# Attention in a fused transformer block: P·V in two halves around the score pairs, and a fourth of the maximum search handed to ScalarE and a scan

## Chip, cores and metric

The kernel runs on one core of a Trainium2 chip, as one program. The metric is the device time of one execution in microseconds (us); lower is better. What is compared is the median of several executions.

## What is computed

The reference is a "macaron" block on x of shape (8, 2048, 256): half a routed feed-forward step, attention, half a routed feed-forward step. The change touches the attention alone, which in the reference is

```python
q = _lowrank(xh, Uq, Vq, bq)
k = _lowrank(xh, Uk, Vk, bk)
v = _lowrank(xh, Uv, Vv, bv)
scores = jnp.einsum('bqhd,bkhd->bhqk', q, k) / DH ** 0.5
attn = jax.nn.softmax(scores, axis=-1)
out = jnp.einsum('bhqk,bkhd->bqhd', attn, v)
```

with 8 batches, 8 heads of 32, and 2048 queries and keys.

## The kernel before

`macaron_block` runs eight stages one after the other. The attention stage `attend` is by far the longest and lies between about 880 and 4370 us of the trace.

**Tiling.** A unit is 512 queries of one group of four heads in one batch. There are 64 units. Within a unit the scores are computed with keys on the partitions and queries along the free dimension, as 16 chunks of 128 keys by four heads: 64 score tiles of 128x512. TensorE writes them into two PSUM banks in turn (`ps_s`), ScalarE takes the exponential of each into `probs` in SBUF, and TensorE multiplies each chunk of four tiles by V into one accumulating bank (`ps_acc`). This last product is called P.V; its four heads are four matmuls that run side by side in four column groups of the array. For chunks 13 and 15 (`RAW_CHUNKS`) TensorE also sums the probabilities into `ps_misc` by a matmul with ones; for the others GpSimd adds them up (`pool_sum`), partly with the help of accumulating DMAs, and one more matmul (`close_z`) adds that sum.

**The maximum.** Softmax subtracts the row maximum before the exponential. It enters the score matmul as an extra row of q, so it must be known a unit ahead. For this the unit's scores are computed once more with queries on the partitions: `max_four` does it for 128 queries, 512 keys and four heads at a time, in four PSUM banks (`ps_max`, one per head), and VectorE reduces the four banks to their maxima (`part_max`). There are 16 such steps per unit, numbered n, run four ahead (`MAX_LEAD`); n modulo 4 is the quarter of the keys, called c in that code. `ps_max` is single, so step n waits until VectorE has finished step n-1 (`part_max_done`), in line 1581.

**The order on TensorE** is written out by hand in `batch`. A unit has 16 cycles, i = 0 to 15, of four score tiles each. This text calls the first two tiles of a cycle A1 and A2, the next two B1 and B2, the maximum step M, and P.V of the previous chunk PV. A cycle is A1, A2, PV, B1, B2, M. Each score tile waits until the exponential of the tile two before it is done, since there are two banks. Some cycles hold more: cycle 3 `close_z`, cycle 4 `turn_z`, cycle 6 `turn_o` (four transposes each), cycle 13 `turn_max`, which takes the place of A2 for a moment. Cycle 0 works off chunk 15 of the unit before.

**ScalarE** takes exponentials in the order of the tiles, and copies `ps_acc` after tile 1 and `ps_misc` after tile 15. **VectorE** does one reduction per cycle (line 1457), a reciprocal in cycle 4 and a normalisation in cycle 6. **GpSimd** adds chunks (line 1437) and starts DMAs that add one chunk to another (line 1414); such a start waits for `pv_done` of the pair's second chunk.

Of the kernel before, what the change touches and what calls it, by code (L numbers as in the profile page):

```python
# [15 lines left out]
P = 128  # L16
# [1196 lines left out]
def attend(nc, tag, qk, v_dram, out):  # L1213
# [6 lines left out]
    FOURS = TILES // HG  # L1220
    BU = NG * NU
# [21 lines left out]
    with ExitStack() as ctx:  # L1243
# [19 lines left out]
        neg_max = sb("neg_max", [P, HG * QT])  # L1263
        max_row = sb("max_row", [HG * QT, P], F32R)
# [19 lines left out]
        part_max_done = sem("part_max_done")  # L1284
        neg_max_done = sem("neg_max_done")
# [159 lines left out]
        def _(dve):  # L1445
# [3 lines left out]

            def part_max_of(unit, n, first_unit=False):  # L1450

                if n == 0 and not first_unit:

                    dve.wait_ge(neg_max_done, unit)
                t, c = divmod(n, QT)
                dve.wait_ge(max_scores, unit * FOURS + n + 1)
                nc.vector.reduce_max(part_max[:, :, t, c], ps_max[:], AX.X).then_inc(part_max_done, 1)  # L1457
                if n == FOURS - 1:
                    dve.wait_ge(part_max_done, unit * FOURS + FOURS)
                    if not first_unit:  # L1460

                        dve.wait_ge(max_turned, unit)
                    nc.vector.tensor_reduce(neg_max[:], part_max[:].rearrange("p h t c -> p (h t) c"), AX.X, ALU.max,
                                            negate=True).then_inc(neg_max_done, 1)
# [47 lines left out]
        def _(act):  # L1512
# [6 lines left out]

            row_of_max(0, 1, first_unit=True)  # L1520

            def batch(b, first_batch=False, last=False):
                for un in range(BU):
# [27 lines left out]
                    for j in range(TILES):  # L1551
                        c, h = divmod(j, HG)
                        if h == 0 and (carry or c >= RING):
                            free(c)
                        act.wait_ge(scores, unit * TILES + j + 1)
                        nc.scalar.activation(probs[:, c % RING, h], ps_s[:, j % 2], ACT.Exp, scale=SCALE  # L1556
                                             ).then_inc(exp_done, 1)
                        if carry and j == 1:
                            copy_acc(unit)
                        if carry and j == CLOSE_Z_IN * PER_CYC + 3:  # L1560
                            copy_z(unit)
                        if j == TURN_MAX_IN * PER_CYC and (un + 1 < BU or not last):
                            row_of_max(unit + 1, 1)
# [11 lines left out]
        def _(pe):  # L1575
            def scores_for_max(unit, un, n, first_unit=False):

                t, c = divmod(n, QT)
                if n >= 1 or not first_unit:

                    pe.wait_ge(part_max_done, unit * FOURS + n)
                for h in range(HG):
# [22 lines left out]
            def batch(b, first_batch=False, last=False):  # L1605
                for un in range(BU):
# [4 lines left out]
                    def pv(n, k, c):  # L1611

                        if c == 0 and carry:

                            pe.wait_ge(oT_done, n)
                        for h in range(HG):
                            last = nc.tensor.matmul(ps_acc[h * DH:(h + 1) * DH, :],  # L1617
                                                    v[:, k // NU, c, h * DH:(h + 1) * DH], probs[:, c % RING, h],
                                                    start=(c == 0), stop=(c == NC - 1))
                        if c in RAW_CHUNKS:  # L1620
                            if c == RAW_CHUNKS[0] and carry:

                                pe.wait_ge(o_done, n)
                            for h in range(HG):
                                last = nc.tensor.matmul(ps_misc[h * DH:(h + 1) * DH, :], ones[:, 0:DH],  # L1625
                                                        probs[:, c % RING, h], start=(c == RAW_CHUNKS[0]), stop=False)
                        last.then_inc(pv_done, 1)

                    def close_z(n, k):

                        pe.wait_ge(pool_added, n * ADDS + ADDS)
                        for h in range(HG):
                            last = nc.tensor.matmul(ps_misc[h * DH:(h + 1) * DH, :], ones[:, 0:DH],
                                                    pool_sum[:, k % 2, h], start=False, stop=True)
                        last.then_inc(z_done, 1)
# [35 lines left out]
                    for i in range(NCYC):  # L1671
# [15 lines left out]
                        if i > 0:  # L1687
                            pv(unit, un, i - 1)
                        elif carry:
                            pv(unit - 1, (un - 1) % BU, NC - 1)  # L1690
                        if carry and i == CLOSE_Z_IN:
                            close_z(unit - 1, un - 1)
                        if turning:
                            pe.wait_ge(max_row_done, unit + 2)
                            score(j + 1)
                        for n in range(2, PER_CYC):

                            pe.wait_ge(exp_done, unit * TILES + j + n - 1)
                            score(j + n)
                        if carry and i == TURN_Z_IN:  # L1700
                            turn_z(unit)
                        if carry and i == TURN_O_IN:
                            turn_o(unit)
                        max_four(i)
                if last:
                    pe.wait_ge(exp_done, (b * BU + BU) * TILES)
                    pv(b * BU + BU - 1, BU - 1, NC - 1)
                    close_z(b * BU + BU - 1, BU - 1)
# [60 lines left out]
```

## Time and profile before

| | us |
|---|---|
| median of 3 executions | 4966.07 (4965.32 to 4968.26) |
| the profiled execution | 4967.85 |
| its span, first to last instruction | 4965.8 |
| TensorE busy in the span | 3964.8 (80%) |
| VectorE busy | 3282.3 (66%) |
| ScalarE busy | 2837.2 (57%) |
| GpSimd busy | 2799.9 (56%) |

The span is divided among stages with different limits. The shares of the whole tell little of the attention stage, in which all the rows below were taken. Matmuls overlap, so what a matmul costs is read from the distance between the starts of neighbours and not from its own duration.

### The profile page before, as it was taken

The numbers are of one execution on the slowest core, as the hardware profiler recorded it, in microseconds if no ns is written. First come the engines' busy times: TensorE is split into PE (matmuls) and PEld (weight loads), VectorE is DVE, ScalarE is ACT, GpSimd is POOL, SyncE is SP. The second block draws the span as 40 slices with busy tenths as digits, with TensorE's granted clock in tenths as the row PEclk, the third lists the DMA queues.
The fourth block names the chain that finished last, engine by engine and source line by source line (L and its number), as shares of the span: only waits on it lengthen the run. The fifth ranks groups of instructions, "written<-read, shape, count | busy, mean of one in ns | idle before, by whom it ended". The sixth has DMA issues, their size and how long they took to land. (4 is left out here: it accounts for less than half of the span.)

```text
span 4965.8 us, 69030 instructions
## 1 busy us (share of the span) xinstructions
PE 3964.8 (80%) x21362; PEld 1556.9 (31%) x21362; DVE 3282.3 (66%) x3736; ACT 2837.2 (57%) x5622; POOL 2799.9 (56%) x966
## 2 busy tenths in 40 slices
PE   0156476599999999999999999999999999910266
PEld 0134354133333333333333333333333333300144
DVE  8744365677767767767776776777677777469644
ACT  4143355266666666666666666666666666623043
POOL 0011000377777877777787777778777777743111
PEclk9999788699999999999999999999999999955598
DMA  6200499557667665756756676675756764566200
GB/s 221 78 26 5 157 352 326 117 110 154 129 143 152 131 143 115 162 125 136 161 121 141 128 158 132 135 157 107 158 125 142 158 128 101 116 197 213 76 5 5
DMA packets 316558, 676.10 MB, mean 136 GB/s; under 512 B 24780, under 2 KB 208608, under 8 KB 268832
## 3 DMA queue, kind: packets, MB, share of 16 engines
q0 software_dynamic: 48000, 340.81, 33.8%
q1 hardware_dynamic: 234624, 297.04, 20.7%
q10 hardware_dynamic: 33568, 33.69, 2.0%
q8 instruction: 191, 3.13, 0.3%
q14 instruction: 175, 1.43, 0.1%
HBM read 198.90 MB, written 136.48 MB: 68 GB/s over the span
## 5 line engine op out<-in xcount | busy, mean ns | idle before, releaser
L1457 DVE TENSOR_REDUCE at_part_max<-at_ps_max 128x4 f32<-128x2048 f32 x1024 | 2348.4, 2293 | 1018.8 <-PE at_ps_max L1584 1017.7
L1556 ACT ACTIVATE at_probs<-at_ps_s 128x512 f32<-128x512 f32 x4096 | 2233.2, 596 | 1044.3 <-PE at_ps_s L1653 988.2
L1437 POOL TENSOR_TENSOR at_pool_sum<-at_pool_sum,at_probs 128x2048 f32<-128x2048 f32 x448 | 2056.5, 4590 | 283.7 <-DMA at_probs<-at_probs 271.0
L1653 PE MATMUL at_ps_s<-at_qs,at_ks 97*128 97x512 f32 (+1 forms) x4096 | 1715.3, 472 | 71.7 <-ACT at_probs L1556 36.3
L1653 PEld LDWEIGHTS at_ps_s<-at_qs,at_ks 97*128 97x128 f32 (+1 forms) x4096 | 682.4, 188 | 1496.0 <-ACT at_probs L1556 1201.0
L1617 PE MATMUL at_ps_acc<-at_probs,at_v 128*32 128x512 f32 x8192 | 1097.0, 608 | 0.9 <-ACT at_probs L1556 0.9
L1584 PE MATMUL at_ps_max<-at_ks,at_qs 32*128 32x512 f32 x4096 | 524.7, 501 | 87.7 <-DVE at_part_max L1457 43.3
L1414 POOL DMA_DIRECT2D at_probs<-at_probs x320 | 282.2, 882 | 498.9 <-PE at_ps_acc L1617 468.7
L1437 POOL TENSOR_TENSOR at_pool_sum<-at_probs 128x2048 f32<-128x2048 f32 x64 | 292.2, 4565 | 97.1 <-ACT at_probs L1556 97.1
L1584 PEld LDWEIGHTS at_ps_max<-at_ks,at_qs 32*128 32x128 f32 x4096 | 198.1, 183 | 442.1 <-DVE at_part_max L1457 296.4
L233 PE MATMUL s_pt<-s_ident,s_sall 128*128 128x128 f32 x2 | 0.9, 446 | 384.1 <-DVE s_sall L202 384.1
L1617 PEld LDWEIGHTS at_ps_acc<-at_probs,at_v 128*32 128x32 f32 x8192 | 161.4, 108 | 256.7 <-issue 247.7
L1394 POOL MEMSET at_ones<- 128x128 f32 x1 | 0.2, 204 | 336.8 <-POOLq L62 336.8
L1182 PE MATMUL pr_pqk<-pr_xT,pr_w 128*128 128x512 f32 x256 | 132.6, 666 | 36.5 <-DVE pr_lo L1085 33.4
L215 ACT ACTIVATE s_y<-s_x,s_small 128x256 f32<-128x256 f32 x256 | 129.2, 587 | 55.4 <-DVE s_small L198 55.4
L175 DVE CUSTOM_DVE_ANT_0 s_junk<-s_x,s_w 128x256 f32<-128x256 f32 x256 | 155.3, 607 | 0.0
L560 POOL TENSOR_TENSOR f_att<-f_att,f_rowsum 128x1280 f32<-128x1280 f32 x16 | 49.5, 3096 | 175.3 <-DVE f_rowsum L645 175.3
L154 POOL TENSOR_TENSOR s_x<-s_x,s_add 128x1024 f32<-128x1024 f32 x32 | 76.7, 2418 | 119.2 <-DMA s_add<-attention 119.2
L1625 PE MATMUL at_ps_misc<-at_probs,at_ones 128*32 128x512 f32 x1024 | 137.1, 607 | 0.0
L747 ACT ACTIVATE f_att<-f_att,f_rowmax 128x128 f32<-128x128 f32 x256 | 98.7, 388 | 45.5 <-DVE f_rowmax L641 45.5
L233 PEld LDWEIGHTS s_pt<-s_ident,s_sall 128*128 128x128 f32 x2 | 0.4, 180 | 384.5 <-issue 384.5
L1141 ACT ACTIVATE pr_hi<-pr_pqk,pr_bias 128x512 fp32r<-128x512 f32 x128 | 83.8, 683 | 60.1 <-PE pr_pqk L1182 59.8
(196 smaller groups left out, 2486.9 us busy)
## 6 DMA issues: line engine op xcount, KB each, us to landing
at_probs<-at_probs POOLq DMA_DIRECT2D x320, 1024.0 KB, 7.3
qk_parts<-pr_hi SPq DMA_DIRECT2D x32, 1024.0 KB, 6.4
qk_parts<-pr_lo SPq DMA_DIRECT2D x32, 1024.0 KB, 6.2
at_qs<-qk_parts SPq DMA_DIRECT2D x320, 64.0 KB, 1.9
at_ks<-qk_parts SPq DMA_DIRECT2D x80, 256.0 KB, 5.6
s_x<-in_x SPq DMA_DIRECT2D x16, 1024.0 KB, 7.6
after_ffn<-s_y ACTq DMA_DIRECT2D x16, 1024.0 KB, 8.4
pr_x<-after_ffn SPq DMA_DIRECT2D x8, 2048.0 KB, 12.4
```

Of the source, the lines that this page charges most:

```text
L175: nc.vector.tensor_tensor_reduce(out=junk[:, t % 4, :], in0=xb[:, k, t, :], in1=w[:], scale=1.0, scalar=0.0, op0=ALU.mult, op1=ALU.add, ac ...
L215: last = nc.scalar.activation(yb[:, k, t, :], xb[:, k, t, :], ACT.Identity, scale=sm[:, k, 0, t:t + 1], bias=sm[:, k, 1, t:t + 1])
L747: last = nc.scalar.activation(att[:, s, h], att[:, s, h], ACT.Exp, scale=ATT_SCALE, bias=rowmax[:, s, h:h + 1], accum_out=rowsum[:, s, h:h ...
L1182: nc.tensor.matmul(pqk[:, m, :], w[:, m // NG, m % NG, :], xT[:, n % 2, m % NG, :], start=True, stop=True).then_inc(qk_done, 1)
L1414: nc.gpsimd.dma_start(probs[:, c % RING], probs[:, a % RING], accum_op=ALU.add).then_inc(dma_added[(un * ND + d) % 2], 16)
L1437: nc.gpsimd.tensor_tensor(acc, a, probs[:, c % RING], ALU.add).then_inc(pool_added, 1)
L1457: nc.vector.reduce_max(part_max[:, :, t, c], ps_max[:], AX.X).then_inc(part_max_done, 1)
L1556: nc.scalar.activation(probs[:, c % RING, h], ps_s[:, j % 2], ACT.Exp, scale=SCALE).then_inc(exp_done, 1)
L1584: last = nc.tensor.matmul(ps_max[:, h], qs[rows, un % NQB, h, t * P:(t + 1) * P], ks[rows, un % BU // NU, h, c * 512:(c + 1) * 512], start ...
L1617: last = nc.tensor.matmul(ps_acc[h * DH:(h + 1) * DH, :], v[:, k // NU, c, h * DH:(h + 1) * DH], probs[:, c % RING, h], start=(c == 0), st ...
L1625: last = nc.tensor.matmul(ps_misc[h * DH:(h + 1) * DH, :], ones[:, 0:DH], probs[:, c % RING, h], start=(c == RAW_CHUNKS[0]), stop=False)
L1653: nc.tensor.matmul(ps_s[:, j % 2], ks[rows, g, h, c * P:(c + 1) * P], qs[rows, un % NQB, h, :], start=True, stop=True).then_inc(scores, 1)
```

## The change

**TensorE.** The maximum step M moves from the end of a cycle to the place behind A2. PV is cut into two halves of 256 query columns: half 0 runs behind M, half 1 behind B2. The matmuls with ones and `close_z` are cut the same way, but the ones that open an accumulation (chunk 0 of P.V, and the ones-product of chunk 13) run whole in half 1. `turn_z` and `turn_o` stand between B2 and half 1. The signal `pv_done` comes with half 1.

**ScalarE.** In cycles whose step has c = 0, 1, 2 it copies one of the four `ps_max` banks (3, 2, 3) to SBUF (`aside`), behind the exponential of A2. `copy_acc` moves from behind tile 1 to behind tile 3.

**VectorE.** It reduces three banks for c = 0 and 3 and two for c = 1 and 2. For c = 1, 2, 3 it then runs a `tensor_tensor_scan` over 512 elements of one bank (3, 2, 3) and the copy set aside from the step before, whose last element is the maximum of both, waits for it, and copies that one element to `part_max`. Where a maximum now stands for two quarters, the other place holds the lowest number, written once at the start.

The core of the diff:

```diff
+    ASIDE = (3, 2, 3, None)
+    MERGED = (None, 3, 2, 3)
...
-                nc.vector.reduce_max(part_max[:, :, t, c], ps_max[:], AX.X).then_inc(part_max_done, 1)
+                banks = HG - 1 if c in (0, QT - 1) else HG - 2
+                last = nc.vector.reduce_max(part_max[:, 0:banks, t, c], ps_max[:, 0:banks], AX.X)
+                h = MERGED[c]
+                if h is not None:
+
+                    dve.wait_ge(aside_done, unit * COPIES + copies_through(n - 1))
+                    nc.vector.tensor_tensor_scan(aside[:, h - 2], ps_max[:, h], aside[:, h - 2], LOWEST, ALU.max, ALU.max
+                                                 ).then_inc(merged, 1)
+                    dve.wait_ge(merged, unit * COPIES + copies_through(n - 1))
+                    last = nc.vector.tensor_copy(part_max[:, h, t, c:c + 1], aside[:, h - 2, 511:512])
+                last.then_inc(part_max_done, 1)
...
+            def set_aside(unit, n):
+
+                c = n % QT
+                if ASIDE[c] is None:
+                    return
+                act.wait_ge(max_scores, unit * FOURS + n + 1)
+                if n > 1:
+
+                    act.wait_ge(part_max_done, unit * FOURS + n - 1)
+                nc.scalar.copy(aside[:, ASIDE[c] - 2], ps_max[:, ASIDE[c]]).then_inc(aside_done, 1)
...
-                        if carry and j == 1:
+                        if j % PER_CYC == 1:
+                            n = j // PER_CYC + MAX_LEAD
+                            ahead = un + 1 + n // FOURS
+                            if ahead < BU or not last:
+                                set_aside(unit + ahead - un, n % FOURS)
+                        if carry and j == PER_CYC - 1:
                             copy_acc(unit)
...
+                if n % QT > 0:
+                    pe.wait_ge(aside_done, unit * COPIES + copies_through(n - 1))
...
+                    def pv_half(n, k, c, half):
+
+                        cols = slice(half * UQ // 2, (half + 1) * UQ // 2)
+                        if c == 0:
+                            if half == 0:
+                                return
+                            cols = slice(0, UQ)
+                            if carry:
+
+                                pe.wait_ge(oT_done, n)
                         for h in range(HG):
...
+                        if half == 1:
+                            last.then_inc(pv_done, 1)
...
-                        for n in range(2, PER_CYC):
-
-                            pe.wait_ge(exp_done, unit * TILES + j + n - 1)
-                            score(j + n)
-                        if carry and i == TURN_Z_IN:
-                            turn_z(unit)
-                        if carry and i == TURN_O_IN:
-                            turn_o(unit)
                         max_four(i)
+                        for half in range(2):
+                            if half == 1:
+                                if turning:
+                                    pe.wait_ge(max_row_done, unit + 2)
+                                    score(j + 1)
+                                for n in range(2, PER_CYC):
+
+                                    pe.wait_ge(exp_done, unit * TILES + j + n - 1)
+                                    score(j + n)
+                                if carry and i == TURN_Z_IN:
+                                    turn_z(unit)
+                                if carry and i == TURN_O_IN:
+                                    turn_o(unit)
+                            if i > 0:
+                                pv_half(unit, un, i - 1, half)
```

TensorE's order in two plain cycles of a unit, before the change (`ps_s` is a pair of score tiles, `ps_acc` P.V, `ps_max` the maximum step; x4 are the four heads):

```order
L1653 MATMUL at_ps_s<-at_qs,at_ks 128x512 x2
L1617 MATMUL at_ps_acc<-at_probs,at_v 32x512 x4
L1653 MATMUL at_ps_s<-at_qs,at_ks 128x512 x2
L1584 MATMUL at_ps_max<-at_ks,at_qs 128x512 x4
L1653 MATMUL at_ps_s<-at_qs,at_ks 128x512 x2
L1617 MATMUL at_ps_acc<-at_probs,at_v 32x512 x4
```

The same place with the change:

```order
L1714 MATMUL at_ps_s<-at_qs,at_ks 128x512 x2
L1630 MATMUL at_ps_max<-at_ks,at_qs 128x512 x4
L1668 MATMUL at_ps_acc<-at_probs,at_v 32x256 x4
L1714 MATMUL at_ps_s<-at_qs,at_ks 128x512 x2
L1668 MATMUL at_ps_acc<-at_probs,at_v 32x256 x4
L1714 MATMUL at_ps_s<-at_qs,at_ks 128x512 x2
L1630 MATMUL at_ps_max<-at_ks,at_qs 128x512 x4
```

The maximum step has moved from behind the second pair to behind the first, and P.V stands as a half at two places.

VectorE's order over four maximum steps (c = 0 to 3) with the change; before, the same four steps are one row, `TENSOR_REDUCE at_part_max<-at_ps_max 128x4 x4`. The row of the scan bears the name of a SCALAR_TENSOR_TENSOR here:

```order
L1472 TENSOR_REDUCE at_part_max<-at_ps_max 128x3 [waits s1_std_ready,s1_stats_done]
L1472 TENSOR_REDUCE at_part_max<-at_ps_max 128x2 [waits s1_std_ready]
L1477 SCALAR_TENSOR_TENSOR at_aside<-at_ps_max,at_aside 128x512 [waits s1_products_done]
L1480 COPY at_part_max<-at_aside 128x1 [waits s1_y_done]
L1472 TENSOR_REDUCE at_part_max<-at_ps_max 128x2 [waits s1_std_ready]
L1477 SCALAR_TENSOR_TENSOR at_aside<-at_ps_max,at_aside 128x512 [waits s1_products_done]
L1480 COPY at_part_max<-at_aside 128x1 [waits s1_y_done]
L1472 TENSOR_REDUCE at_part_max<-at_ps_max 128x3 [waits s1_std_ready]
L1477 SCALAR_TENSOR_TENSOR at_aside<-at_ps_max,at_aside 128x512 [waits s1_products_done]
L1480 COPY at_part_max<-at_aside 128x1 [waits s1_y_done]
```

The waits are printed with names of an earlier stage that used the same semaphores; their places are what counts: the copy waits for the scan. Four instructions of VectorE, one per step, have become ten.

## Rows read from the trace of the kernel before

**Rows 1.** The page: busy us, share of the span, instructions of each engine.

```profile
PE 3964.8 (80%) x21362; PEld 1556.9 (31%) x21362; DVE 3282.3 (66%) x3736; ACT 2837.2 (57%) x5622; POOL 2799.9 (56%) x966
```

**Rows 2.** Busy time by window: us, busy (x) per engine, PEclk, DMA share, GB/s.

```profile
1000.00:4280.00 3280.00, 3206.39 (x17763) 1112.60 (x17759) 2315.49 (x1169) 2204.29 (x4119) 2501.80 (x799) 1.00 0.64 136
```

**Rows 3.** Groups, 1000 to 4280 us: xcount | busy us, mean ns | idle before, releaser.

```profile
L1457 DVE TENSOR_REDUCE at_part_max<-at_ps_max 128x4 f32<-128x2048 f32 x984 | 2256.7, 2293 | 963.9 <-PE at_ps_max L1584 962.9
L1556 ACT ACTIVATE at_probs<-at_ps_s 128x512 f32<-128x512 f32 x3935 | 2145.6, 596 | 991.8 <-PE at_ps_s L1653 936.3 <-POOL at_pool_sum L1437 0.2
L1437 POOL TENSOR_TENSOR at_pool_sum<-at_pool_sum,at_probs 128x2048 f32<-128x2048 f32 x430 | 1974.2, 4591 | 276.0 <-DMA at_probs<-at_probs 264.3
```

**Rows 4.** Timeline, weight loads, one plain cycle: start us, us, instruction, [idle before].

```profile
2508.49 0.16 PEld L1617 LDWEIGHTS at_ps_acc<-at_probs,at_v 128*32 128x32 f32 x8 [0.33 <-issue]
2509.49 0.30 PEld L1653 LDWEIGHTS at_ps_s<-at_qs,at_ks 97*128 97x128 f32 x2 [0.84 <-ACT at_probs L1556]
2510.31 0.19 PEld L1584 LDWEIGHTS at_ps_max<-at_ks,at_qs 32*128 32x128 f32 x4 [0.52 <-DVE at_part_max L1457]
2510.75 0.19 PEld L1653 LDWEIGHTS at_ps_s<-at_qs,at_ks 97*128 97x128 f32 x1 [0.24 <-ACT at_probs L1556]
2511.17 0.19 PEld L1653 LDWEIGHTS at_ps_s<-at_qs,at_ks 97*128 97x128 f32 x1 [0.23 <-ACT at_probs L1556]
2511.60 0.16 PEld L1617 LDWEIGHTS at_ps_acc<-at_probs,at_v 128*32 128x32 f32 x8 [0.24 <-issue]
```

**Rows 5.** Timeline of ScalarE in the same cycle.

```profile
2510.03 1.08 ACT L1556 ACTIVATE at_probs<-at_ps_s 128x512 f32<-128x512 f32 x2 [0.57 <-PE at_ps_s L1653]
```

**Rows 6.** Timeline of VectorE, two neighbouring maximum steps.

```profile
2507.97 2.29 DVE L1457 TENSOR_REDUCE at_part_max<-at_ps_max 128x4 f32<-128x2048 f32 x1 [1.25 <-PE at_ps_max L1584]
...
2510.87 2.29 DVE L1457 TENSOR_REDUCE at_part_max<-at_ps_max 128x4 f32<-128x2048 f32 x1 [0.45 <-PE at_ps_max L1584]
```

**Rows 7.** Timeline of TensorE, cycle 3 with the closing sum (line 1633).

```profile
2501.36 1.06 PE L1617 MATMUL at_ps_acc<-at_probs,at_v 128*32 128x512 f32 x8
2502.24 1.04 PE L1633 MATMUL at_ps_misc<-at_pool_sum,at_ones 128*32 128x512 f32 x8
2503.21 0.73 PE L1653 MATMUL at_ps_s<-at_qs,at_ks 97*128 97x512 f32 x2
2503.87 0.50 PE L1584 MATMUL at_ps_max<-at_ks,at_qs 32*128 32x512 f32 x4
```

**Rows 8.** Timeline of TensorE, cycle 6: second pair, four transposes, maximum step.

```profile
2512.60 0.74 PE L1653 MATMUL at_ps_s<-at_qs,at_ks 97*128 97x512 f32 x2
...
2513.70 0.51 PE L1584 MATMUL at_ps_max<-at_ks,at_qs 32*128 32x512 f32 x4
```

**Rows 9.** Timeline of TensorE, cycle 13, in which the maximum is turned.

```profile
2532.46 0.50 PE L1653 MATMUL at_ps_s<-at_qs,at_ks 97*128 97x512 f32 x1
...
2533.16 1.07 PE L1617 MATMUL at_ps_acc<-at_probs,at_v 128*32 128x512 f32 x8
2534.16 0.73 PE L1653 MATMUL at_ps_s<-at_qs,at_ks 97*128 97x512 f32 x2
2535.34 0.50 PE L1653 MATMUL at_ps_s<-at_qs,at_ks 128*128 128x512 f32 x1 [0.45 <-ACT at_probs L1556]
2535.77 0.51 PE L1584 MATMUL at_ps_max<-at_ks,at_qs 32*128 32x512 f32 x4
```

**Rows 10.** Groups of VectorE over the whole span, shapes apart.

```profile
L1485 DVE TENSOR_TENSOR at_o<-at_ps_misc,at_rz 128x512 f32<-128x512 f32 x64 | 43.6, 681 | 7.2 <-PE at_ps_misc L1647 7.2
...
L629 DVE TENSOR_TENSOR f_kspread<-f_ps,f_head_of 128x1024 f32<-128x1024 f32 x32 | 36.6, 1217 | 26.6 <-PE f_ps L815 26.6
```

**Rows 11.** Single lines: duration ns min/median/max, first and last start us.

```profile
L186 DVE TENSOR_SCALAR s_small<-s_small x32: 171/171/2206, 14.7 to 4594.5; 128x8 f32<-128x8 f32 x32
L1463 DVE TENSOR_REDUCE at_neg_max<-at_part_max x64: 219/220/221, 930.7 to 4293.9; 128x16 f32<-128x64 f32 x64
```

**Rows 12.** Timeline of GpSimd: end of one unit's sum, and a DMA start.

```profile
2492.25 9.21 POOL L1437 TENSOR_TENSOR at_pool_sum<-at_pool_sum,at_probs 128x2048 f32<-128x2048 f32 x2 [1.32 <-DMA at_probs<-at_probs]
...
2516.48 0.86 POOL L1414 DMA_DIRECT2D at_probs<-at_probs  x1 [5.03 <-PE at_ps_acc L1617]
```

More of the change, by code:

```diff
@@ L1616, in pv @@
                         for h in range(HG):
-                            last = nc.tensor.matmul(ps_acc[h * DH:(h + 1) * DH, :],
-                                                    v[:, k // NU, c, h * DH:(h + 1) * DH], probs[:, c % RING, h],
-                                                    start=(c == 0), stop=(c == NC - 1))
+                            last = nc.tensor.matmul(ps_acc[h * DH:(h + 1) * DH, cols],
+                                                    v[:, k // NU, c, h * DH:(h + 1) * DH], probs[:, c % RING, h, cols],
+                                                    start=(c == 0),
+                                                    stop=(c == NC - 1 and half == 1))
@@ L1620, in pv @@
                         if c in RAW_CHUNKS:
-                            if c == RAW_CHUNKS[0] and carry:
-                                pe.wait_ge(o_done, n)
-                            for h in range(HG):
[L1625 to L1631, printed above, removed]
+                            first = c == RAW_CHUNKS[0]
@@ new lines, in pv_half @@
+                            if first and half == 0:
+                                return
+                            if first:
+                                cols = slice(0, UQ)
+                                if carry:
+                                    pe.wait_ge(o_done, n)
+                            for h in range(HG):
+                                last = nc.tensor.matmul(ps_misc[h * DH:(h + 1) * DH, cols], ones[:, 0:DH],
+                                                        probs[:, c % RING, h, cols], start=first, stop=False)
@@ L1632, in close_z @@
+                        if half == 1:
+                            last.then_inc(pv_done, 1)
+                    def close_z(n, k, half):
+                        cols = slice(half * UQ // 2, (half + 1) * UQ // 2)
+                        if half == 0:
+                            pe.wait_ge(pool_added, n * ADDS + ADDS)
                         for h in range(HG):
-                            last = nc.tensor.matmul(ps_misc[h * DH:(h + 1) * DH, :], ones[:, 0:DH],
-                                                    pool_sum[:, k % 2, h], start=False, stop=True)
@@ L1635, in close_z @@
-                        last.then_inc(z_done, 1)
+                            last = nc.tensor.matmul(ps_misc[h * DH:(h + 1) * DH, cols], ones[:, 0:DH],
+                                                    pool_sum[:, k % 2, h, cols], start=False, stop=(half == 1))
+                        if half == 1:
+                            last.then_inc(z_done, 1)
                     def turn_z(n):
@@ L1705, in batch @@
                 if last:
                     pe.wait_ge(exp_done, (b * BU + BU) * TILES)
-                    pv(b * BU + BU - 1, BU - 1, NC - 1)
-                    close_z(b * BU + BU - 1, BU - 1)
+                    for half in range(2):
+                        pv_half(b * BU + BU - 1, BU - 1, NC - 1, half)
+                    for half in range(2):
+                        close_z(b * BU + BU - 1, BU - 1, half)
                     turn_z(b * BU + BU)
```

30 lines of the change are left out of this document (18 added, 12 removed).

## The prediction

> **What bounds the kernel now.** The page comes first: TensorE is busy 80% of the span, VectorE 66%, ScalarE 57% [rows 1]. The window from 1000 to 4280 us then shows that in attention TensorE is busy 3206 of 3280 us at granted clock 1.00, the 2.4 GHz level [rows 2]. That looks like a TensorE bound, but matmuls overlap, so I read the timeline of one plain cycle instead. The groups give the mean cycle: 984 maximum steps in 3280 us are 3.33 us each, 53.3 us per unit of 16 [rows 3].
>
> In the plain cycle P.V starts at 2508.49 and again at 2511.60: 3.11 us [rows 4]. Its parts, from weight load to weight load:
> - B1 at 2509.49. Its exponential starts at 2510.03, and both exponentials of the pair end at 2511.11 [rows 5]. A2 of the next cycle needs the second one, and starts at 2511.17. B1 to A2 is 1.68.
> - A2 to P.V: 0.43. P.V to B1: 1.00. Sum 3.11 [rows 4].
>
> This is the loop that sets a plain cycle: score, two exponentials, score, P.V. The maximum step is in the shadow of the 1.68. VectorE has a loop of its own: M at 2510.31, reduction from 2510.87 [rows 4, 6], that is 0.56; the reduction 2.29; and 0.05 from its end (2507.97 + 2.29 = 2510.26) to the next M at 2510.31. Together 2.90, which is 0.2 below 3.11. VectorE's 963.9 us of waiting in the window [rows 3] is therefore one small slack per cycle plus the long cycles, and a longer VectorE step costs nothing until it passes 2.5 us.
>
> **TensorE's plain cycle after the change.** Its chain is B1 to A2 1.68, A2 to M 0.43, M 0.44 (2510.31 to 2510.75), half 0 of P.V, then B1. The half has no row. P.V whole takes 1.00, of which the first weight load, 0.11, does not shrink (0.16 for eight loads started 0.007 apart); the rest halves: 0.11 + 0.89/2 = 0.56. Its bounds are 0.50 (half of all) and 1.00 (nothing saved). The chain is 1.68 + 0.43 + 0.44 + 0.56 = 3.11. The step that left the shadow is as long as the half that went into it, so a plain cycle gains nothing. Half 1 is hidden: B pair 0.66 (2503.21 to 2503.87 [rows 7]) + 0.56 + 0.11 for A1 = 1.33 < 1.68. The price of the move is that M now lies on the chain: every delay of M, which was in the shadow, is paid in full.
>
> **ScalarE's copies.** A copy costs at most an exponential, 0.60 [rows 3], in a row with others 0.49 (1.08 for two less 0.60). It stands behind A2's exponential; ScalarE is then free some 0.3 us before B1's scores arrive. Hidden, as long as that gap lasts.
>
> **VectorE's new steps.** Reductions follow the size: 512 elements from PSUM 0.68, 1024 1.22 [rows 10], 2048 2.29 [rows 3], so three banks (1536) are 1.75 and two are 1.22. The scan has no row. Its lower bound is a two-input instruction over 512, 0.68. As upper bound I take 1024 elements, 1.22: each element passes two maximum operations in series, and the next element needs the result of the second, so it may take two slots instead of one. I take 1.22, for that reason; the reduction, which runs at one slot, sends its state through a single operation, and speaks for the lower end. A copy of one element is at most the 0.17 of an eight-element instruction [rows 11]; with the wait for the scan 0.20. Then:
> - c = 0: 1.75 + 0.61 of hand-over = 2.36. Not binding.
> - c = 1, 2: 1.22 + 1.22 + 0.20 + 0.61 = 3.25, which is 0.14 over 3.11.
> - c = 3: 1.75 + 1.22 + 0.20 + 0.61 = 3.78, which is 0.67 over.
>
> VectorE's work over four steps goes from 9.2 to 1.75 + 2.64 + 2.64 + 3.17 = 10.2 us: the relief in banks (16 to 10) is spent on three scans.
>
> The Trainium skill has a rule on exactly this: "DVE: opcode table, instruction layouts, handler registers and perf-mode slots", section "Datapath and trigger behaviour", says that the built-in tensor_tensor_scan feeds its result back to an earlier stage and runs at half throughput. By it the scan over 512 costs like 1024, the sum below; at full throughput it would be rival 1. No row here shows a scan.
>
> **The long cycles.** Before, 53.3 less 16 x 3.11 leaves 3.5 us per unit. They are: three groups of ones-products, 1.85 - 1.00 = 0.85 each (2501.36 to 2503.21 [rows 7]), 2.6; the turning cycle, whose first score starts at 2532.46 and whose M ends at 2535.77 + 0.44, 0.64; the rest, some 0.3, are turns and loads. After:
> - Chunks 13 and 15: the part in half 0 is on the chain (0.43), the part in half 1 overruns the shadow (0.66 + 0.56 + 0.43 + 0.11 - 1.68 = 0.08); chunk 13's whole product in half 1 overruns it by 0.51. So 0.51 each, 1.0; the closing sum falls on a c = 3 step and is swallowed there.
> - Cycle 1 has no half 0 (chunk 0 runs whole in half 1, hidden), but ScalarE is late there: the copy of the accumulator, the two exponentials and the copy set aside stand in a row. I work out +0.2.
> - Cycle 4: transposes add 0.44 (1.10 instead of 0.66 [rows 8]) ahead of half 1: +0.1, and 0.15 for the copy of `ps_misc`. In cycle 6 they hide within 0.1.
> - Cycle 13: M comes 0.70 behind A1 (as P.V did, 2532.46 to 2533.16), 0.2 earlier than in a plain cycle. From there M 0.44, half 0.56, A2; B2 1.18 later (2534.16 to 2535.34 [rows 9]); the copy set aside pushes B's exponentials 0.3 back; A2 to the next A2 is 2.67, M another 0.43: 4.10, which is 0.99 over. Net +0.78.
> - VectorE: four c = 3 steps, 4 x 0.67 = 2.7; of the eight others, the five not in a long cycle, 0.7.
> - Loads and rest 0.3.
>
> Sum per unit: 16 x 3.11 = 49.8, + 1.0 + 0.2 + 0.25 + 0.78 + 2.7 + 0.7 + 0.3 = 55.7, against 53.3: +2.4. Times 63 units 151, plus some 5 for the twenty steps ahead of the first unit, which VectorE alone paces (mean 3.16 instead of 2.90). The profiled execution, 4967.85, becomes 5124; it lies 1.8 above the median of the runs, which gives 5122, and I round to **5125 us**.
>
> **GpSimd** hangs on `pv_done`, which now comes with half 1, 0.66 + 0.56 = 1.2 us later. Its DMA start waited 5.03 us for P.V at 2516.48, and the unit's last addition ends at 2501.46 while its reader, the closing sum, starts at 2502.24 [rows 7, 12]: there is little room. With cycles lengthened by VectorE the chain gets about that time back; without (rival 1) the closing sum waits up to 1 us per unit.
>
> **The rivals.**
> 1. *The scan runs at full rate* (0.69). c = 3 becomes 3.25, c = 1, 2 2.72. Of VectorE's 3.4 remain 0.4, but the closing sum costs 0.5 again, and up to 1 us waits for GpSimd: +0 to +1 per unit, 4968 to 5030, say 4995. For it: the reduction's one slot per element. Against: two operations in the loop. 15%.
> 2. *Faster:* full rate, and TensorE need not empty between M and its neighbours. A2 to P.V takes 0.43 although a pair's second score follows its first after about 0.24 (0.66 - 0.43). If M followed A2 at that distance, the chain would be 2.92, and some ten cycles save 0.19: 1.9 per unit, minus the 0.4 above: 4870. It decides only if VectorE's step stays below 2.3, thus never with the slow scan. Against: P.V behind A2, and M behind B2, both show the full distance. The Trainium skill agrees, in "TensorEngine Tiling (Array Packing)", section "Key Properties": a change of tiling mode drains TensorE. 10%.
> 3. *The one-element copy is held up by GpSimd.* Line 186, a one-input SBUF instruction of 0.17, once took 2.2 us; line 1463, a reduction from SBUF in the midst of GpSimd's additions, never did (219 to 221 ns) [rows 11]. GpSimd is busy 76% of the window. A copy that must wait loses half an addition, 0.76 x 2.3 = 1.7 us, twelve times a unit, less as the unit grows: +15 per unit, 5900. 4%.
> 4. *A half costs as much as the whole* (0.9 to 1.0): the chain is 3.5, +6.5 per unit, 5400. 5%.
>
> **How the numbers follow.** Forecast 66%, rivals 15, 10, 4 and 5%. The forecast's own range, from terms of 0.05 us per step, is 5070 to 5210. With rival 1 the range is 4975 to 5230, which holds 8 in 10. A measurement of this kernel tells 0.2% (10 us) from no change. Faster: rival 2 and a little of rival 1, 12%. Same: a third of rival 1, 5%. Slower: the rest, 83%.
>
> **What would show it.** The scan's mean duration: 1.2 confirms the main step, 0.7 is rival 1. VectorE's steps with c = 3 should lie 3.8 apart, TensorE's M should wait for VectorE, and VectorE should be busy about 2.55 us per step, idle less than the 0.98 of now. Plain cycles (behind c = 0) should stay at 3.1. A one-element copy above 0.2 is rival 3. I am wrong if the distance from half 0 to B1 is not near 0.56, or from A2 to M not 0.43.

## The result

The changed kernel takes 5110.48 us (median of 4 executions, 5106.0 to 5123.69) against 4966.24 for the kernel before: ratio 1.0293, 95% interval 1.0277 to 1.0308. It is slower by 144 us; the time lies 15 us below the forecast 5125. The profiled execution below is the longest of the four, 5123.69, span 5121.9; its terms are compared with the sum made against the profiled execution before, which gave 5124. It lies 13 us above its own median, at a mean granted clock of 0.927 against 0.931 to 0.932 in the other three, so its unit is about 0.2 us longer than that of a median run.

The page of the changed kernel, busy us by engine, to be read beside [rows 1]:

```profile
PE 4042.1 (79%) x30066; PEld 1731.0 (34%) x30066; DVE 3448.7 (67%) x5273; ACT 3223.5 (63%) x6390; POOL 2810.1 (55%) x966
```

TensorE's and VectorE's shares are almost the same as before, and ScalarE's has risen from 57 to 63%; they would not tell which engine became slower. The groups of the attention stage, 1000 to 4400 us, do (shape, xcount | busy us, mean ns | idle before, releaser):

```profile
L1477 DVE TENSOR_TENSOR_SCAN at_aside<-at_ps_max,at_aside 128x512 f32<-128x512 f32 x734 | 889.4, 1212 | 0.0
L1472 DVE TENSOR_REDUCE at_part_max<-at_ps_max 128x3 f32<-128x1536 f32 x489 | 860.1, 1759 | 323.9 <-PE at_ps_max L1630 318.2
L1472 DVE TENSOR_REDUCE at_part_max<-at_ps_max 128x2 f32<-128x1024 f32 x488 | 598.2, 1226 | 584.1 <-PE at_ps_max L1630 584.1
L1630 PE MATMUL at_ps_max<-at_ks,at_qs 32*128 32x512 f32 x3908 | 496.7, 496 | 99.1 <-DVE at_part_max L1480 90.2
L1553 ACT COPY at_aside<-at_ps_max 128x512 f32<-128x512 f32 x732 | 432.4, 591 | 66.3 <-PE at_ps_max L1630 66.3
L1480 DVE COPY at_part_max<-at_aside 128x1 f32<-128x1 f32 x734 | 112.7, 154 | 25.5
```

The scan over 512 elements takes 1.21 us, as long as the 1024 elements of [rows 10]. 489 + 488 steps in 3400 us are 3.48 us each, 55.7 us per unit, which is the forecast sum. VectorE is busy 2.52 us per step (forecast 2.55) and idle 0.96 (before 0.98). TensorE's matmuls now stand idle before M for VectorE's one-element copy, 90 us in the window; in [rows 4] M came between the pairs, and its wait of 0.52 us for VectorE was in the shadow.

The hand-over from VectorE to TensorE behind c = 3 shows in the timeline (start us, us, engine, instruction, [idle before]). M, three rows of VectorE, then the next M:

```profile
2518.46 0.19 PEld L1630 LDWEIGHTS at_ps_max<-at_ks,at_qs 32*128 32x128 f32 x4 [0.37 <-issue]
...
2519.02 1.76 DVE L1472 TENSOR_REDUCE at_part_max<-at_ps_max 128x3 f32<-128x1536 f32 x1 [1.24 <-PE at_ps_max L1630]
...
2520.69 1.21 DVE L1477 TENSOR_TENSOR_SCAN at_aside<-at_ps_max,at_aside 128x512 f32<-128x512 f32 x1
...
2521.94 0.15 DVE L1480 COPY at_part_max<-at_aside 128x1 f32<-128x1 f32 x1
2522.15 0.19 PEld L1630 LDWEIGHTS at_ps_max<-at_ks,at_qs 32*128 32x128 f32 x4 [0.82 <-DVE at_part_max L1480]
```

From M to M 3.69 (forecast 3.78): 0.56, then 1.67 to the scan's start, 1.25 to the copy's, 0.21 to M. TensorE's weight load waits 0.82 of it.

Behind c = 0 VectorE is early, and the step shows TensorE's own chain. Weight loads, changed kernel:

```profile
2549.72 0.19 PEld L1630 LDWEIGHTS at_ps_max<-at_ks,at_qs 32*128 32x128 f32 x4 [0.82 <-DVE at_part_max L1480]
2550.16 0.16 PEld L1668 LDWEIGHTS at_ps_acc<-at_probs,at_v 128*32 128x32 f32 x8 [0.25 <-issue]
2550.73 0.30 PEld L1714 LDWEIGHTS at_ps_s<-at_qs,at_ks 97*128 97x128 f32 x2 [0.41 <-issue]
2551.40 0.16 PEld L1668 LDWEIGHTS at_ps_acc<-at_probs,at_v 128*32 128x32 f32 x8 [0.37 <-issue]
2551.97 0.19 PEld L1714 LDWEIGHTS at_ps_s<-at_qs,at_ks 97*128 97x128 f32 x1 [0.41 <-ACT at_probs L1595]
2552.41 0.19 PEld L1714 LDWEIGHTS at_ps_s<-at_qs,at_ks 97*128 97x128 f32 x1 [0.25 <-ACT at_probs L1595]
2552.84 0.19 PEld L1630 LDWEIGHTS at_ps_max<-at_ks,at_qs 32*128 32x128 f32 x4 [0.24 <-issue]
```

The rows are M, half 0, the pair B, half 1, A1, A2 and the next M. M takes 0.44, half 0 0.57, B1 to A2 1.68 (2550.73 to 2552.41), A2 to M 0.43: 3.12. The pairs, the halves and the wait of A2 for ScalarE stand as worked out; the plain cycle is no shorter than [rows 4].

### The profile page after: what moved, and what is told of

It reads as the page before. It is cut to its first block and busy times, and to the rows that moved or that the text cites. A ratio compares the mean times of both kernels' runs of the same rounds, so it can differ in the third digit from the quotient of the medians.

```text
span 5121.9 us, 90932 instructions
## 1 busy us (share of the span) xinstructions
PE 4042.1 (79%) x30066; PEld 1731.0 (34%) x30066; DVE 3448.7 (67%) x5273; ACT 3223.5 (63%) x6390; POOL 2810.1 (55%) x966
## 3 DMA queue, kind: packets, MB, share of 16 engines
q14 instruction: 205, 1.68, 0.1%
## 5 line engine op out<-in xcount | busy, mean ns | idle before, releaser
L1448 POOL TENSOR_TENSOR at_pool_sum<-at_pool_sum,at_probs 128x2048 f32<-128x2048 f32 x448 | 2079.0, 4641 | 237.5 <-DMA at_probs<-at_probs 222.6
L1472 DVE TENSOR_REDUCE at_part_max<-at_ps_max 128x3 f32<-128x1536 f32 (+1 forms) x1024 | 1528.2, 1492 | 982.2 <-PE at_ps_max L1630 976.4
L1714 PE MATMUL at_ps_s<-at_qs,at_ks 97*128 97x512 f32 (+1 forms) x4096 | 1673.6, 470 | 53.4 <-ACT at_probs L1595 29.7
L1668 PE MATMUL at_ps_acc<-at_probs,at_v 128*32 128x256 f32 (+1 forms) x15872 | 1307.7, 401 | 0.1
L1714 PEld LDWEIGHTS at_ps_s<-at_qs,at_ks 97*128 97x128 f32 (+1 forms) x4096 | 669.7, 189 | 1151.5 <-ACT at_probs L1595 983.8
L1477 DVE TENSOR_TENSOR_SCAN at_aside<-at_ps_max,at_aside 128x512 f32<-128x512 f32 x768 | 930.5, 1212 | 0.0
L1553 ACT COPY at_aside<-at_ps_max 128x512 f32<-128x512 f32 x768 | 453.6, 591 | 152.7 <-PE at_ps_max L1630 152.2
L1668 PEld LDWEIGHTS at_ps_acc<-at_probs,at_v 128*32 128x32 f32 x15872 | 313.6, 108 | 578.3 <-issue 577.4
L1682 PE MATMUL at_ps_misc<-at_probs,at_ones 128*32 128x256 f32 (+1 forms) x1536 | 147.6, 457 | 0.0
L1480 DVE COPY at_part_max<-at_aside 128x1 f32<-128x1 f32 x768 | 117.9, 154 | 26.7
```

The source lines that it names most:

```text
L1448: nc.gpsimd.tensor_tensor(acc, a, probs[:, c % RING], ALU.add).then_inc(pool_added, 1)
L1472: last = nc.vector.reduce_max(part_max[:, 0:banks, t, c], ps_max[:, 0:banks], AX.X)
L1477: nc.vector.tensor_tensor_scan(aside[:, h - 2], ps_max[:, h], aside[:, h - 2], LOWEST, ALU.max, ALU.max).then_inc(merged, 1)
L1553: nc.scalar.copy(aside[:, ASIDE[c] - 2], ps_max[:, ASIDE[c]]).then_inc(aside_done, 1)
L1668: last = nc.tensor.matmul(ps_acc[h * DH:(h + 1) * DH, cols], v[:, k // NU, c, h * DH:(h + 1) * DH], probs[:, c % RING, h, cols], start=(c ...
L1682: last = nc.tensor.matmul(ps_misc[h * DH:(h + 1) * DH, cols], ones[:, 0:DH], probs[:, c % RING, h, cols], start=first, stop=False)
```

## The experiments

All times are medians; ratios are to the kernel before, run on the same chip. "Steps" are maximum steps in the window from 1000 to 4200 us, from the groups of VectorE; 3200 us divided by them and times 16 is the unit.

**Only TensorE's order** (e_order). VectorE's step is one reduction again, and nothing is set aside; ScalarE's `copy_acc` stays where the change put it:

```diff
-                banks = HG - 1 if c in (0, QT - 1) else HG - 2
-                last = nc.vector.reduce_max(part_max[:, 0:banks, t, c], ps_max[:, 0:banks], AX.X)
...
+                nc.vector.reduce_max(part_max[:, :, t, c], ps_max[:], AX.X).then_inc(part_max_done, 1)
...
-                        if j % PER_CYC == 1:
...
-                                set_aside(unit + ahead - un, n % FOURS)
```

> Only the order on TensorE of the change (the maximum step behind A2, P.V and the ones-products in halves), with VectorE's single reduction over four banks as before and no copies set aside. My theory: a plain cycle is 2.11 us plus the larger of the two groups of matmuls that stand between the pairs (behind A: M 0.44 + half 0.56 = 1.00; behind B: half 0.56), so 3.11, as before; VectorE's loop of 2.90 does not bind. Long cycles are some 1.1 us per unit shorter (ones-products 0.5 instead of 0.85 each, cycle 1 and 13 shorter), of which GpSimd, released 1.2 us later, may take back up to 1 us. Time 4900 to 4966, say 4920. Rival: the order itself costs time (a half costs more than 0.56, or leaving the shadow costs M's whole 0.44 per cycle): 5050 or more.

Measured 4999.72 (4982.15 to 5008.46), ratio 1.0061 (1.0040 to 1.0083). Plain cycles are 3.11, but there is a loss of 34 us where I expected a gain of 46. Waits in the window 1000 to 4280 (engine, who waited for whom: us in total, times, longest), kernel before and then this one:

```profile
PEld at_ps_misc L1633 <- POOL at_pool_sum L1437: 4.7, 6, 2.3
```

```profile
PEld at_ps_misc L1672 <- POOL at_pool_sum L1448: 26.1, 21, 3.9
```

GpSimd's last addition comes late for the closing sum. That is part of the loss; e_order_late shows how much of it, and that the gain does not appear without these waits either.

**Only the work of VectorE and ScalarE** (e_scan). TensorE's order is that of the kernel before, so M is in the shadow and P.V whole; the copy set aside stands behind the exponential of the next A1:

```diff
+                        if j % PER_CYC == 0:
+                            n = j // PER_CYC + MAX_LEAD - 1
...
+                                set_aside(unit + ahead - un, n % FOURS)
...
                     pe.wait_ge(part_max_done, unit * FOURS + n)
+                if n % QT > 0:
+                    pe.wait_ge(aside_done, unit * COPIES + copies_through(n - 1))
```

> Only the work of VectorE and ScalarE of the change (copies set aside, reductions over two or three banks, scan, one-element copy), with TensorE's order as before: M behind B2, in the shadow of the exponentials, and P.V whole. My theory: VectorE's loops are 2.36, 3.25, 3.25 and 3.78 us for c = 0 to 3, in all 12.64 against 4 x 3.11 = 12.44, and since M has slack here a late step can be caught up in the c = 0 cycle: a loss of 1 to 2 us per unit, 5020 to 5090, say 5050. Rival: the place of M makes no difference and the scan's cost shows in full: 5110, as with the whole change.

Measured 5115.92, ratio 1.0298 (1.0281 to 1.0315): the rival's number, the same as the whole change. The loss of the change is the loss of this part. My reason for less, that M could catch up in its shadow, does not hold. Weight loads behind a c = 3 step:

```profile
2372.90 0.19 PEld L1630 LDWEIGHTS at_ps_max<-at_ks,at_qs 32*128 32x128 f32 x4 [1.29 <-DVE at_part_max L1480]
2373.33 0.30 PEld L1699 LDWEIGHTS at_ps_s<-at_qs,at_ks 97*128 97x128 f32 x2 [0.24 <-issue]
2374.00 0.16 PEld L1663 LDWEIGHTS at_ps_acc<-at_probs,at_v 128*32 128x32 f32 x8 [0.36 <-issue]
2374.99 0.19 PEld L1699 LDWEIGHTS at_ps_s<-at_qs,at_ks 97*128 97x128 f32 x1 [0.84 <-ACT at_probs L1595]
2375.50 0.19 PEld L1699 LDWEIGHTS at_ps_s<-at_qs,at_ks 128*128 128x128 f32 x1 [0.33 <-ACT at_probs L1595]
2375.93 0.19 PEld L1630 LDWEIGHTS at_ps_max<-at_ks,at_qs 32*128 32x128 f32 x4 [0.24 <-issue]
```

The step behind has c = 0. When M comes late, everything behind it on TensorE is late too: M 0.43, pair 0.67, P.V 0.99, pair 0.94 (its second score waits for an exponential that ScalarE's copy pushed back). That is 3.03 to the next M, only 0.08 less than a plain cycle, though VectorE had needed 2.36. Slack against one's own loop is no slack where the queue behind the waiting instruction is nearly full.

**The scan at full rate** (e_fullrate):

```diff
-                    nc.vector.tensor_tensor_scan(aside[:, h - 2], ps_max[:, h], aside[:, h - 2], LOWEST, ALU.max, ALU.max
-                                                 ).then_inc(merged, 1)
+                    nc.vector.tensor_tensor(aside[:, h - 2], ps_max[:, h], aside[:, h - 2], ALU.max).then_inc(merged, 1)
```

> The whole change, with the scan over 512 elements replaced by an elementwise maximum of the same two operands into the same place, so that the element copied on is not the maximum: that part of the computation is changed. It shows the change at an instruction of 0.68 us instead of 1.21. My theory: VectorE's loops become 2.36, 2.72, 2.72, 3.25 and stop binding but for 0.14 at c = 3; 4968 to 5030, say 4990. Rival: the loss lies in TensorE's order or in ScalarE's copies: it stays above 5070.

Measured 4984.89, ratio 1.0038 (1.0024 to 1.0053). The group of VectorE, 1000 to 4200 us:

```profile
L1477 DVE TENSOR_TENSOR at_aside<-at_ps_max,at_aside 128x512 f32<-128x512 f32 x714 | 486.1, 681 | 0.0
```

The element copied on is not the maximum here; this kernel leaves that part of the computation out. 0.53 us less per scan, 12 scans per unit, took 126 us off: all but 19 us of the loss. ScalarE's copies, the one-element copies and the halves are still there, so none of them is the cause of these 126 us. The 19 us were not taken apart; the closing sum's weight loads wait 15.4 us for GpSimd in the window.

**P.V cut at 128 columns** (e_cut128). The kernel is e_order with another cut. The loop of the prediction, written with the two groups of matmuls between the pairs, is 2.11 us (1.68 + 0.43) plus the group behind A, and by symmetry 2.11 plus the group behind B. If that holds, the halves are the wrong cut: with M on one side, 128 and 384 columns make both groups equal.

```diff
+CUT = 128
...
-                        cols = slice(half * UQ // 2, (half + 1) * UQ // 2)
+                        cols = (slice(0, CUT), slice(CUT, UQ))[half]
```

> The order of the change without scan and copies, and P.V cut at 128 instead of 256 columns: part 0 is 128 columns behind M, part 1 is 384 behind B2. My theory (2.11 plus the larger group): behind A 0.44 + 0.33 = 0.77, behind B 0.78, so 2.89, just at VectorE's loop of 2.90: a plain cycle of 2.9 instead of 3.1. The ones-products and transposes behind B now cost their full 0.6 and 0.4, some 4.1 us of long cycles; unit 50.5 to 51, time about 4805 (4780 to 4850). Rival: the distribution does not matter, only the sum of TensorE's work and VectorE's loop do: as e_order, 4920.

Measured 4986.69, ratio 1.0039 (1.0028 to 1.0049). The plain cycle did what was worked out, the time did not. Weight loads from M to M:

```profile
2505.00 0.19 PEld L1610 LDWEIGHTS at_ps_max<-at_ks,at_qs 32*128 32x128 f32 x4 [0.37 <-DVE at_part_max L1472]
2505.44 0.16 PEld L1648 LDWEIGHTS at_ps_acc<-at_probs,at_v 128*32 128x32 f32 x8 [0.25 <-issue]
2505.79 0.40 PEld L1694 LDWEIGHTS at_ps_s<-at_qs,at_ks 97*128 97x128 f32 x2 [0.20 <-issue]
2506.45 0.16 PEld L1648 LDWEIGHTS at_ps_acc<-at_probs,at_v 128*32 128x32 f32 x8 [0.26 <-issue]
2507.23 0.42 PEld L1694 LDWEIGHTS at_ps_s<-at_qs,at_ks 97*128 97x128 f32 x2 [0.62 <-ACT at_probs L1582]
2507.91 0.19 PEld L1610 LDWEIGHTS at_ps_max<-at_ks,at_qs 32*128 32x128 f32 x4 [0.25 <-DVE at_part_max L1472]
```

2.91 us. The last M waited for VectorE, whose own loop is 2.90 by [rows 4, 6], so here two limits meet and 2.91 alone does not tell them apart; e_cut384 does. TensorE's matmuls from the same cycle on:

```profile
2506.45 0.85 PE L1648 MATMUL at_ps_acc<-at_probs,at_v 128*32 128x384 f32 x8
2507.23 0.74 PE L1694 MATMUL at_ps_s<-at_qs,at_ks 97*128 97x512 f32 x2
2507.91 0.50 PE L1610 MATMUL at_ps_max<-at_ks,at_qs 32*128 32x512 f32 x4
2508.34 0.43 PE L1648 MATMUL at_ps_acc<-at_probs,at_v 128*32 128x128 f32 x8
2512.87 0.43 PE L1673 MATMUL at_ps_misc<-at_pool_sum,at_ones 128*32 128x128 f32 x8 [4.11 <-POOL at_pool_sum L1449]
2513.23 1.22 PE L1694 MATMUL at_ps_s<-at_qs,at_ks 97*128 97x512 f32 x2
2514.38 1.51 PE L1648 MATMUL at_ps_acc<-at_probs,at_v 128*32 128x384 f32 x8
```

The matmuls follow one another without idle time up to the closing sum, which waits 4.1 us for GpSimd. In the window such waits are 68.1 us. That GpSimd is late because its starts hang on the end of P.V, and because the shorter cycles gave it less time, is argued and not measured apart.

**The same with the closing sum two cycles later** (e_cut128_late, e_order_late):

```diff
-CLOSE_Z_IN = 3
-TURN_Z_IN = 4
-TURN_O_IN = 6
+CLOSE_Z_IN = 5
+TURN_Z_IN = 6
+TURN_O_IN = 8
```

> As e_cut128, with the closing sum in cycle 5, the transposes of z in 6 and of the output in 8 instead of 3, 4 and 6. In e_cut128 a plain cycle took 2.91 as worked out, but TensorE stood 68 us in the window before the closing sum and waited for GpSimd's last addition. My theory: two cycles more of room (5.8 us against a longest wait of 5.1) take these waits away and nothing else: 4987 - 70 = 4915 (4900 to 4935). Rival: GpSimd's chain of additions and DMAs is as long as the unit, and the wait only moves: 4975 or more.

Measured 4910.42 (4899.45 to 4913.75), ratio 0.9890 (0.9873 to 0.9906), which is faster than both kernels: 56 us below the kernel before, 200 below the changed one. Waits for the last addition are down from 68.1 to 8.9 us, 59 less; the time fell by 76, and the other 17 were not taken apart. GpSimd's room does not make up the whole miss of e_cut128, though: 4910 is still 105 above the 4805 worked out there. 978 steps in 3200 us give a unit of 52.4 where I had 50.5 to 51. The plain steps are 2.91, so the long cycles cost 5.8 us per unit above 16 plain ones, and not 4.1.

> As e_order, with the closing sum and both turns two cycles later. e_order's waits for GpSimd's last addition were 26 us in the window. Theory: they go, 5000 - 27 = 4973 (4960 to 4980). Rival: the 34 us by which e_order is slower than the kernel before come from the halves themselves, and the late closing changes nothing: 5000.

Measured 4968.87, ratio 1.0006 (0.9997 to 1.0016). The order of the change, given room for GpSimd, is worth nothing and costs nothing. Its long cycles are not shorter than before, as I had said for e_order: 49 of the 80 us between 4920 and 5000 are that miss, and only 31 are GpSimd.

**The late closing alone** (e_late): the same three constants in the kernel before.

> The kernel before with only the closing sum and the two turns two cycles later (5, 6, 8). It is the control for e_cut128_late. Theory: the kernel before waited 4.7 us in its window for GpSimd's last addition, so nothing is to be gained: 4955 to 4970. Rival: the late closing is itself the gain of e_cut128_late: below 4930.

Measured 4966.88, ratio 1.0005 (0.9995 to 1.0014). So the gain of e_cut128_late is that of the cut, released by the late closing.

**P.V whole, behind B** (e_whole): the kernel before with M and P.V exchanged.

```diff
-                        if carry and j == 1:
+                        if carry and j == PER_CYC - 1:
                             copy_acc(unit)
...
+                        max_four(i)
+                        if turning:
...
+                            score(j + n)
...
                         if i > 0:
                             pv(unit, un, i - 1)
...
-                        max_four(i)
```

> The kernel before with M behind A2 and P.V whole behind B2 (ones-products and closing sum with it), one reduction over four banks, no halves, no scan. The pair A is then followed by 0.44 and the pair B by 1.00. Theory: only the larger group counts, whichever pair it follows, so a plain cycle stays at 3.11; with P.V 1.7 us later GpSimd's chain costs some waits: 4966 to 5030, say 4990. Rival: with M ahead of the long group, M's 0.44 adds to the chain (3.5 per cycle): above 5300.

Measured 5069.83, ratio 1.0210 (1.0193 to 1.0227): neither number. Its weight loads show where:

```profile
2503.29 0.19 PEld L1653 LDWEIGHTS at_ps_s<-at_qs,at_ks 128*128 128x128 f32 x1 [0.30 <-ACT at_probs L1556]
2503.42 0.57 PEld L1647 LDWEIGHTS at_ps_misc<-at_ident,at_oT 128*128 128x128 f32 x4
2504.15 0.16 PEld L1617 LDWEIGHTS at_ps_acc<-at_probs,at_v 128*32 128x32 f32 x8 [0.17 <-issue]
2505.15 0.30 PEld L1653 LDWEIGHTS at_ps_s<-at_qs,at_ks 97*128 97x128 f32 x2 [0.84 <-ACT at_probs L1556]
2505.81 0.19 PEld L1584 LDWEIGHTS at_ps_max<-at_ks,at_qs 32*128 32x128 f32 x4 [0.37 <-issue]
...
2508.90 0.19 PEld L1584 LDWEIGHTS at_ps_max<-at_ks,at_qs 32*128 32x128 f32 x4 [0.37 <-DVE at_part_max L1457]
```

The step from 2505.81 to 2508.90 is a plain one and takes 3.09, as the theory has it: it does not matter which pair the larger group follows. But the transposes of the cycles 4 and 6 now share the side of P.V, the long one, and are paid in full, 0.44 each (a score to P.V is 0.86 from 2503.29 to 2504.15, and 0.42 from 2506.82 to 2507.24 without them); I had left them out. With 934 steps the unit is 54.8, which is 1.5 above 53.3. Two transposes explain 0.9 of it, and the rest, in the cycles of the ones-products and of the turn, I did not take apart.

**The cut at 384** (e_cut384), as e_cut128 with `CUT = 384`:

> As e_cut128 with the cut at 384: M and 384 columns behind A2, 128 behind B2. Theory (2.11 plus the larger group, 0.44 + 0.78 = 1.22): a plain cycle of 3.33, some 2.4 us per unit above e_order: 5120 to 5170. Rival: the cut does not matter: 5000.

One execution, 5108.47, somewhat below what I had worked out. Its plain step is 3.32 us, where 2.11 + 1.22 is 3.33, and M does not wait for VectorE:

```profile
2529.59 0.19 PEld L1610 LDWEIGHTS at_ps_max<-at_ks,at_qs 32*128 32x128 f32 x4 [0.24 <-issue]
...
2532.91 0.19 PEld L1610 LDWEIGHTS at_ps_max<-at_ks,at_qs 32*128 32x128 f32 x4 [0.24 <-issue]
```

920 steps give a unit of 55.7, and the order of the times follows the larger group: 0.78 gives 4987 (4910 with room), 1.00 gives 5000 (4969), 1.22 gives 5108.

**The whole change with the cut at 128** (e_cut128_scan):

> The whole change with P.V cut at 128 instead of 256 columns. Theory: behind c = 1, 2 and 3 VectorE's loops (3.22, 3.22, 3.69 us in the changed kernel) set the step whatever TensorE has to do, and only steps behind c = 0 can fall from 3.11 to 2.9: 4 x 0.2 per unit less the dearer closing cycle, 5060 to 5100. Rival: TensorE's chain sets the changed kernel, and the cut brings what it brought between e_order and e_cut128_late, some 50 to 90 us: below 5050.

Measured 5089.04, ratio 1.0254 (1.0237 to 1.0271): 21 us below the changed kernel. While the scan is there, VectorE hides what the better cut gives.

**One chunk more for GpSimd** (e_pool13), as e_cut128_late with

```diff
-RAW_CHUNKS = (13, 15)
+RAW_CHUNKS = (15,)
```

> As e_cut128_late, with the ones-product of chunk 13 left out on TensorE (0.86 us per unit) and chunk 13 added by GpSimd instead (one more addition of 4.6 us per unit). Theory: in e_cut128_late GpSimd is no longer idle for lack of P.V (2.4 us per unit), only waiting for its own DMAs (8.7 us per unit), and is about as long as the unit of 52.4: the addition makes it the bound, 4930 to 5050, say 4980. Rival: TensorE's work alone sets the unit, 0.86 x 62 = 53 less: 4857.

Measured 5147.81, ratio 1.0363 (1.0341 to 1.0386). The direction is right, the size is not. Busy by window, 1000 to 4280 us (as [rows 2]), and a wait:

```profile
1000.00:4280.00 3280.00, 3046.81 (x23842) 1248.93 (x23845) 2196.27 (x1107) 2100.09 (x3907) 2634.35 (x816) 0.95 0.63 131
```

```profile
PEld at_ps_misc L1673 <- POOL at_pool_sum L1449: 177.1, 50, 5.6
```

GpSimd is busy 80% of it and the closing sum waits again, 50 times. The granted clock is down to 0.95, against 0.99 in e_cut128_late. GpSimd's waits for its DMAs did not shrink when it got more to do, though I had counted on that: 530.5 us in 3280, against 536.3 in 3200 of e_cut128_late. So GpSimd has no room for one addition more. It is not the only limit of the fastest version: there M's weight load waits for VectorE in many plain cycles (592 times in the window, 169.6 us), whose loop of 2.90 is as long as the cycle.

## Why the prediction was right

**The plain cycle.** Right to 0.01 us, in both directions of test: 3.11 stays 3.11 or 3.12 when P.V is cut in halves, becomes 3.32 when the larger group grows to 1.22, and 2.91 when the groups are equal, which is also where VectorE's loop lies. That this chain and not TensorE's busy share sets the cycle was argued ahead; e_cut384 shows it, with the same matmuls as e_order and VectorE not in the way.

**VectorE.** The term that decides. The scan took 1.21 (taken 1.22), the copy 0.15 (0.17), three banks 1.76 (1.75); c = 3 steps 3.69 (3.78), since the scan starts 0.09 before the end of the reduction (2520.69 against 2519.02 + 1.76 above). e_scan alone gives the whole loss, e_fullrate takes 126 of the 144 us away. The Trainium skill's sentence in "DVE: opcode table, instruction layouts, handler registers and perf-mode slots", section "Datapath and trigger behaviour", that the scan runs at half throughput, agrees with this trace: 1212 ns against 681 ns for an elementwise instruction of the same size, and 1217 ns for one of twice the size [rows 10].

**The long cycles.** Mostly right. Cycle 13 and the one behind it were worked out as 2.9 and 4.10; M starts at 2507.70, 2510.59 and 2514.69 in the changed kernel, so 2.89 and 4.10:

```profile
2507.70 0.51 PE L1630 MATMUL at_ps_max<-at_ks,at_qs 32*128 32x512 f32 x4 [0.51 <-DVE at_part_max L1480]
...
2510.59 0.51 PE L1630 MATMUL at_ps_max<-at_ks,at_qs 32*128 32x512 f32 x4
...
2514.69 0.51 PE L1630 MATMUL at_ps_max<-at_ks,at_qs 32*128 32x512 f32 x4
```

Two terms were too small. The steps behind the ones-products take 3.77 (2514.69 to the M at 2518.46) and not 3.62. Where A1 and A2 are both ready, the pair takes 0.66 up to the next kind of matmul; I had put A2's weight load 0.11 behind A1 and added the 0.43 of a lone score, which is 0.54. 0.15 twice a unit is 19 us. And the transposes of cycle 6 do not hide within 0.1: in e_order, where VectorE's loop of 2.90 does not bind, the distance from M to M over them has a median of 3.33 in the window, 0.22 over a plain one. Together these are the 0.5 us per unit that the sum lacks: the terms without VectorE's, with 0.5 for the closing sum, add up to 52.8, while e_order_late has 53.3, as before the change.

**The exact hit is partly luck.** VectorE's steps were taken too long, c = 3 by 0.09 and c = 1, 2 by 0.03, some 0.4 per unit or 25 us. That cancels the terms above, and 5124 against 5123.69 compares with an execution 13 us above its median. The mechanism does not hang on it: what the scan adds is 130 us by the forecast (5125 less the 4995 of rival 1) and 126 by e_fullrate.

**GpSimd.** I said that it hangs on P.V with little room, and that cycles lengthened by VectorE give the time back. The changed kernel shows no wait of the closing sum for it in its window, e_order shows 26 us of them and e_cut128 68, which fits both.

**The rivals.** Rival 1 falls with the scan's 1212 ns; it was given as 4995 for the full rate, and e_fullrate ran at 4985. Rival 2 needed M to follow A2 at 0.24 us; the loads above have 0.43 from A2 to M (2552.41 to 2552.84) and 0.44 from M to half 0. Rival 3: the one-element copy takes 153 to 156 ns in all its 768 instances, while GpSimd is busy 73% of the window, so it is not held up. Rival 4: a part costs 0.57 (256 columns), 0.35 (128) and 0.78 (384), as a fixed 0.11 to 0.13 and the rest by columns.

**What I had wrong in the experiments.** e_pool13, and 31 us of e_order and 76 of e_cut128, missed because GpSimd, which was not on the chain before, had less room than its idle time suggests. The larger part of both, 49 and 105 us, is that I took the long cycles too short, and so is the miss of e_whole. e_scan missed because slack that I took from one engine's loop was already used by the queue behind it; that is a reading of one late step, which the equal times of e_scan and the whole change support.

## What to carry to other kernels

In this kernel TensorE and ScalarE hand tiles to and fro through two buffers, and the plain cycle was the hand-over (2.11 us) plus the larger of the two groups of other matmuls between the pairs: 3.11 with groups of 1.00 and 0.57, 3.32 with 1.22 and 0.35. Where such a loop is the limit, cut and place work so that the groups are equal, not so that the pieces are; and cost the long cycles as carefully as the plain one, for they held the larger misses here. Before work is taken off an engine, ask what the replacement costs per element: here 6 of 16 banks taken off were paid with three scans that cost two banks each. And an engine that is off the chain by a microsecond can come onto it as soon as the chain gets shorter. Moving its reader back cost nothing here (e_late, 4967), and e_cut128 shows its gain only with it.

## What was not expected of the hardware

After a wait of 4.1 us of TensorE in e_cut128, its matmuls ran at about half speed for a while: the part with 384 columns takes 0.85 us at 2506.45 and 1.51 us at 2514.38, in the rows above. The granted clock is 1.00, the 2.4 GHz level, from 2504 to 2508 and 0.50, the 1.2 GHz level, from 2513.3 to 2516.5; it is back at 1.00 from 2517 on. So a wait for GpSimd there costs more than its own length; what the lower clock adds in all was not measured.

e_order (4982 to 5008) and e_cut128 (4975 to 4992) also vary more from one execution to the next than the kernel before on the same chip (4962 to 4971). e_order_late does so too (4960 to 4977), though its profile shows no wait of the closing sum for GpSimd, so the cause of the spread stays open.
